# Attention with one ones-burst per block: pair sums folded by accumulating transfers

## The chip, the cores and the metric

The kernel runs on one core of one Trainium2 chip. The metric is the device time of that core in microseconds, from the start of the program to its end, as the median of several runs. The engines that matter here are TensorE (PE, matmuls into PSUM), ScalarE (ACT, exponentials and copies out of PSUM), VectorE (DVE, row maxima), GpSimd (POOL, sums of SBUF tiles) and SyncE (SP, which issues the transfers). Each engine runs its own instruction stream in order; they meet only through semaphores.

## What is computed

The reference is a state-space layer with a feed-forward layer, followed by one attention layer on x of shape (2, 2048, 512). The change touches only the attention, of which this is the core (16 heads of 32 columns, B = 2, N = 2048, D = 512):

```python
qkv = (h @ Wqkv.T + bqkv).reshape(B, N, num_heads, hd, 3)
q = jnp.moveaxis(qkv[..., 0], 2, 1)
k = jnp.moveaxis(qkv[..., 1], 2, 1)
v = jnp.moveaxis(qkv[..., 2], 2, 1)
energy = jnp.einsum('bhqd,bhkd->bhqk', q, k)
att = jax.nn.softmax(energy, axis=-1) / D ** 0.5
out = jnp.einsum('bhqk,bhkd->bhqd', att, v)
```

A softmax divides by the sum of the exponentials over all 2048 keys. How the kernel gets that sum is what is changed.

## The kernel before

The program is a series of stages with a barrier between them: preparation, state space, feed-forward, the projections to q, k and v, the attention, and the output projection. In the attention stage a *block* is 512 queries (CH) of one batch entry for a group of four heads (HG = 4). There are 4 groups x 2 entries x 4 chunks = 32 blocks. A block walks through 16 key *tiles* of 128 keys (NKT), and for each tile through four heads. `it` and `n` number the blocks: four blocks (n) to an iteration, eight iterations.

The work of a block, as it is spread over the engines:

- **TensorE** runs `one`. For each tile it does four `score` matmuls (keys x queries, 512 columns, L1554) into three PSUM banks in turn, and between them up to five `search` matmuls (L1540, three other banks) of the *following* block, whose row maxima have to be known before its scores. SHARES gives 4 searches in tile 0, 5 in tiles 1 to 12 and none in tiles 13 to 15 (here called the tail). Two tiles later (AV_LAG) it runs `weigh`, a burst of four matmuls (L1565), which multiplies the probabilities of a tile with the values. After every second tile it runs `total`, a burst of four matmuls with a tile of ones (L1575), which sums one pair of tiles over its 128 keys and accumulates in the PSUM bank DEN. Both bursts work on 32 output columns a head, in f32.
- **ScalarE** takes the exponential of each score bank into `probs` (L1650), eight buffers of four heads x 512. A buffer is free when `weigh` and the pair sum of its tile are done (`av_ready`, `pair_ready`). It also copies the two results, `o_sum` (L1632) and `den` (L1637), once a block.
- **GpSimd** adds the two `probs` tiles of a pair into `pair` (L1711), eight times a block, with two `pair` buffers; an add waits until `total` has read the buffer (`sums_ready`).
- **VectorE** reduces each search bank to row maxima (L1673, 64 a block), finishes the maxima, and in the tail inverts `den` (L1681) and multiplies it into `o_sum` (L1685).
- **SyncE** loads keys, values and queries of later blocks, the negated maxima (four small transfers of `load_max_rows`, L1062, which the first score of the next block waits for) and stores the results.

The order on each engine is the order of the code. `blocks` (L1432) runs block 0, then a hardware loop (`Fori`) of seven iterations with four blocks each, then the last three blocks; SyncE has a loop of its own over the groups. Waits inside the loops compare a semaphore with a count taken from the loop's register.

Of the kernel before, what the change touches and what calls it, by code (L numbers as in the profile page):

```python
# [6 lines left out]
P = 128  # L7
# [3 lines left out]
HEADS, HD = 16, 32  # L11
HG = P // HD
NG = HEADS // HG
CH = 512
# [1366 lines left out]
def attention_stage(nc, sb, sem, psum, a, wp, first, q_dram, k_dram, v_dram, att_dram):  # L1381
# [10 lines left out]
    NKT = L // P  # L1392
# [6 lines left out]
    NPROB = 8  # L1399
# [3 lines left out]
    AV_LAG, SUM_LAG = 2, 5  # L1403
# [7 lines left out]
    pair = [sb(f"pair{n}", [P, HG, CH]) for n in range(2)]  # L1411
# [9 lines left out]
    av_ready, pair_ready, sums_ready = sem("av_ready"), sem("pair_ready"), sem("sums_ready")  # L1421
# [10 lines left out]
    def blocks(engine, block):  # L1432

        block(0, 0, True, False)
        with engine.Fori(0, ITERS - 1) as it:
            for n in range(1, NB):
                block(it, n, False, False)
            block(it + 1, 0, False, False)
        for n in range(1, NB):
            block(ITERS - 1, n, False, n == NB - 1)  # L1440

    with nc.Block() as block:
        @block.sync
        def _(sp):
# [76 lines left out]
            group(0, True, False)  # L1521
            with sp.Fori(1, NG - 1) as g:
                group(g, False, False)
            group(NG - 1, False, True)
# [5 lines left out]
        def _(pe):  # L1530
# [12 lines left out]
            def score(it, n, kt, h):  # L1543

                if kt == 0 and h == 0:

                    pe.wait_ge(q_ld[n], (Q_LD + ROW_LD) * (it + 1))
                unit = UNITS * n + HG * kt + h

                if unit >= 3:  # L1550
                    pe.wait_ge(exp_ready, NB * UNITS * it + unit - 2)
                elif not (n == 0 and isinstance(it, int)):
                    pe.wait_ge(exp_ready, NB * UNITS * it)
                nc.tensor.matmul(psum[:, SC + unit % 3, :], keys[n // PB][0:R + 1, h, kt * P:(kt + 1) * P], queries[n][0:R + 1, h, :],  # L1554
                                 start=True, stop=True).then_inc(sc_ready, 1)

            def weigh(it, n, kt):

                tile = NKT * (NB * it + n) + kt
                pe.wait_ge(exp_ready, HG * (tile + 1))  # L1560
                if kt == 0:
                    pe.wait_ge(o_copied, NB * it + n + 1)
                    pe.wait_ge(v_ld[n // PB], 16 * (it // PER_GROUP + 1))
                for h in range(HG):
                    mm = nc.tensor.matmul(psum[h * HD:(h + 1) * HD, OUT, :], values[n // PB][:, kt, h * HD:(h + 1) * HD], probs[kt % NPROB][:, h, :],  # L1565
                                          start=(kt == 0), stop=(kt == NKT - 1))
# [17 lines left out]

            def pair_of(it, n, kt):

                return it, n, kt // 2

            def one(it, n, first, last):
                following = (it, n + 1) if n < NB - 1 else (it + 1, 0)  # L1590
                j = iter(() if last else range(MAXES))
                for kt in range(NKT):
# [21 lines left out]
                    if (kt - SUM_LAG) % 2 == 0 and (kt >= SUM_LAG or not first):  # L1614
                        total(*pair_of(*lagged(it, n, kt, SUM_LAG)))
# [4 lines left out]
            for kt in range(NKT + 1, NKT + SUM_LAG, 2):  # L1620
                total(ITERS - 1, NB - 1, (kt - SUM_LAG) // 2)

        @block.scalar
        def _(act):
# [9 lines left out]
            def copy_sums(count):  # L1634

                act.wait_ge(sums_ready, PAIRS * (count + 1))
                act.activation(den[:, :], psum[:, DEN, :], ACT.Copy).then_inc(den_copied, 1)  # L1637

            def one(it, n, first, last):
                count = NB * it + n  # L1640
                for kt in range(NKT):
                    tile = NKT * count + kt
                    if kt >= NPROB or not first:

                        act.wait_ge(av_ready, tile - NPROB + 1)
                        act.wait_ge(pair_ready, PAIRS * count + (kt - NPROB) // 2 + 1)
                    for h in range(HG):
                        act.wait_ge(sc_ready, HG * tile + h + 1)
                        unit = UNITS * n + HG * kt + h
                        act.activation(probs[kt % NPROB][:, h, :], psum[:, SC + unit % 3, :], ACT.Exp).then_inc(exp_ready, 1)  # L1650
                    if not first:
                        if kt == AV_LAG - 1:
                            copy_out(count - 1)
                        if kt == SUM_LAG - 1:
                            copy_sums(count - 1)
# [347 lines left out]
```

## Time and profile before

| | |
|---|---|
| median of 3 runs | 3516.28 us (3515.79 to 3516.89) |
| span of the profiled execution | 3515.4 us |
| mean granted TensorE clock | 0.966 of full speed |
| the attention stage in it | about 1452 to 3352 us |
| TensorE busy | 3268.0 us (93% of the span) |
| VectorE, ScalarE, GpSimd busy | 63%, 44%, 45% |

The profiled execution is 0.9 us under the median, so its durations can be set against the runs as they are. The busy time of TensorE is a modelled one, since matmuls are pipelined and overlap; for what a piece costs, the distance from one start to the next is the better measure. A block's length can be read as the distance between two copies of `o_sum` on ScalarE, of which there is one a block. A single `score` or `search` is 0.24 us from start to start in the dense part.

### The profile page before, as it was taken

The numbers are of one execution on the slowest core, as the hardware profiler recorded it, in microseconds if no ns is written. First come the engines' busy times: TensorE is split into PE (matmuls) and PEld (weight loads), VectorE is DVE, ScalarE is ACT, GpSimd is POOL, SyncE is SP. The second block draws the span as 40 slices with busy tenths as digits, with TensorE's granted clock in tenths as the row PEclk, the third lists the DMA queues.
The fourth block names the chain that finished last, engine by engine and source line by source line (L and its number), as shares of the span: only waits on it lengthen the run. The fifth ranks groups of instructions, "written<-read, shape, count | busy, mean of one in ns | idle before, by whom it ended". The sixth has DMA issues, their size and how long they took to land. (4 is left out here: it accounts for less than half of the span.)

```text
span 3515.4 us, 52215 instructions
## 1 busy us (share of the span) xinstructions
PE 3268.0 (93%) x16326; PEld 1933.5 (55%) x16326; DVE 2212.9 (63%) x3513; ACT 1553.0 (44%) x2770; POOL 1567.1 (45%) x538
## 2 busy tenths in 40 slices
PE   4786999999997989899999999999999999999976
PEld 2675777777875767544444444444444444444355
DVE  7884222222215446577778787777787777878558
ACT  2322232322222222465556555555555555655632
POOL 2665111100012111366566566666665565666655
PEclk8897999999998999999999999999999999999988
DMA  6233100000003463500122110122001230100044
GB/s 245 73 122 105 43 24 24 12 12 24 25 12 126 174 189 120 148 22 13 26 61 58 29 25 13 40 50 61 22 13 26 61 73 14 25 13 7 4 150 155
DMA packets 119434, 214.40 MB, mean 61 GB/s; under 512 B 11719, under 2 KB 29147, under 8 KB 118794
## 3 DMA queue, kind: packets, MB, share of 16 engines
q1 hardware_dynamic: 119180, 211.20, 20.0%
q8 instruction: 136, 2.23, 0.3%
q14 instruction: 118, 0.97, 0.1%
HBM read 135.34 MB, written 75.53 MB: 60 GB/s over the span
## 5 line engine op out<-in xcount | busy, mean ns | idle before, releaser
L1711 POOL TENSOR_TENSOR pair<-probs 128x2048 f32<-128x2048 f32 x256 | 1174.5, 4588 | 786.6 <-PE psum L1575 720.8
L1673 DVE TENSOR_REDUCE part_max<-psum 128x1 f32<-128x512 f32 x1984 | 1244.8, 685 | 387.8 <-PE psum L1540 387.8
L1650 ACT ACTIVATE probs<-psum 128x512 f32<-128x512 f32 x2048 | 1090.5, 599 | 787.0 <-PE psum L1554 786.5
L1554 PE MATMUL psum<-queries,keys 97*128 97x512 f32 x2048 | 817.8, 419 | 25.9 <-issue 11.8
L1540 PE MATMUL psum<-keys,queries 96*128 96x512 f32 x1984 | 834.0, 421 | 4.9 <-DMA queries<-q_parts 4.9
L1540 PEld LDWEIGHTS psum<-keys,queries 96*128 96x128 f32 x1984 | 377.5, 190 | 427.3 <-DVE part_max L1673 360.7
L1554 PEld LDWEIGHTS psum<-queries,keys 97*128 97x128 f32 x2048 | 378.4, 190 | 403.7 <-ACT probs L1650 332.6
L1565 PE MATMUL psum<-probs,values 128*32 128x512 f32 x4096 | 548.8, 608 | 0.0
L980 DVE TENSOR_TENSOR h_lo<-w_stage,h_hi 128x512 fp32r<-128x512 f32 x128 | 96.7, 756 | 528.4 <-ACT h_hi L918 528.4
L911 ACT ACTIVATE w_stage<-psum,b_col 128x512 f32<-128x512 f32 x128 | 88.2, 689 | 510.5 <-PE psum L38 510.5
L1024 POOL TENSOR_TENSOR ffn_u_lo<-ffn_u,ffn_u_hi 128x512 fp32r<-128x512 f32 x32 | 41.2, 1288 | 554.1 <-DVE ffn_u_hi L970 554.1
L1575 PE MATMUL psum<-pair,att_ones 128*32 128x512 f32 x2048 | 272.7, 605 | 2.2 <-POOL pair L1711 2.2
L36 PE MATMUL psum<-ffn_u_hi,w_hi 128*128 128x512 f32 x512 | 204.0, 398 | 6.4 <-DVE b_parts L1006 6.4
L36 PE MATMUL psum<-w_hi,h_hi 128*128 128x512 f32 x512 | 203.5, 398 | 0.0
L38 PE MATMUL psum<-ffn_u_lo,w_hi 128*128 128x512 f32 x512 | 203.0, 396 | 0.0
L37 PE MATMUL psum<-w_hi,h_lo 128*128 128x512 f32 x512 | 202.9, 396 | 0.0
L37 PE MATMUL psum<-ffn_u_hi,w_lo 128*128 128x512 f32 x512 | 202.9, 396 | 0.0
L38 PE MATMUL psum<-w_lo,h_hi 128*128 128x512 f32 x512 | 202.3, 395 | 0.0
L1565 PEld LDWEIGHTS psum<-probs,values 128*32 128x32 f32 x4096 | 80.9, 108 | 161.0 <-issue 88.5
L1371 POOL TENSOR_TENSOR qkv_u_lo<-qkv_u,qkv_u_hi 128x512 fp32r<-128x512 f32 x32 | 41.2, 1287 | 263.5 <-DVE qkv_u_hi L1316 263.5
L1681 DVE RECIPROCAL den<-den 128x512 f32<-128x512 f32 x32 | 107.2, 3350 | 47.1 <-ACT den L1637 47.1
L1337 DVE SCALAR_TENSOR_TENSOR qk_lo<-psum,bqkv_col,qk_hi 128x512 fp32r<-128x512 f32 x64 | 47.9, 750 | 118.7 <-ACT qk_hi L1266 118.7
(305 smaller groups left out, 3708.0 us busy)
## 6 DMA issues: line engine op xcount, KB each, us to landing
queries<-q_parts SPq DMA_DIRECT2D x96, 256.0 KB, 4.7
keys<-k_parts SPq DMA_DIRECT2D x42, 512.0 KB, 7.3
x<-in_x_dram SPq DMA_DIRECT2D x8, 1024.0 KB, 8.1
y<-in_x_dram SPq DMA_DIRECT2D x8, 1024.0 KB, 6.4
y_rows<-y SPq DMA_DIRECT2D x8, 1024.0 KB, 4.8
qkv_z<-z_rows SPq DMA_DIRECT2D x8, 1024.0 KB, 5.8
q_parts<-qk_hi SPq DMA_DIRECT2D x32, 256.0 KB, 2.0
q_parts<-qk_lo SPq DMA_DIRECT2D x32, 256.0 KB, 2.3
```

Source lines behind the costliest of these rows:

```text
L36: nc.tensor.matmul(out, w_hi, x_hi, start=first, stop=False)
L37: nc.tensor.matmul(out, w_lo, x_hi, start=False, stop=False)
L38: return nc.tensor.matmul(out, w_hi, x_lo, start=False, stop=last)
L980: dve.tensor_tensor(h_lo[j % NH][:, :], g[j % 2], h_hi[j % NH][:, :].bitcast(F32), ALU.subtract).then_inc(glo_ready, 1)
L1540: nc.tensor.matmul(psum[:, MX + j % 3, :], queries[n][0:R, h, qt * P:(qt + 1) * P], keys[n // PB][0:R, h, kc * CH:(kc + 1) * CH], start=Tr ...
L1554: nc.tensor.matmul(psum[:, SC + unit % 3, :], keys[n // PB][0:R + 1, h, kt * P:(kt + 1) * P], queries[n][0:R + 1, h, :], start=True, stop= ...
L1565: mm = nc.tensor.matmul(psum[h * HD:(h + 1) * HD, OUT, :], values[n // PB][:, kt, h * HD:(h + 1) * HD], probs[kt % NPROB][:, h, :], start= ...
L1575: mm = nc.tensor.matmul(psum[h * HD:(h + 1) * HD, DEN, :], ones[:, :], pair[p % 2][:, h, :], start=(p == 0), stop=(p == PAIRS - 1))
L1650: act.activation(probs[kt % NPROB][:, h, :], psum[:, SC + unit % 3, :], ACT.Exp).then_inc(exp_ready, 1)
L1673: dve.tensor_reduce(part_max[:, at, kc:kc + 1], psum[:, MX + j % 3, :], AX.X, ALU.max).then_inc(max_read, 1)
L1681: dve.reciprocal(den[:, :], den[:, :]).then_inc(inverted, 1)
L1711: pool.tensor_tensor(pair[p % 2][:, :, :], probs[2 * p % NPROB][:, :, :], probs[(2 * p + 1) % NPROB][:, :, :], ALU.add).then_inc(pair_read ...
```

## The change

The ones-matmuls are no longer done per pair. GpSimd still adds the two tiles of a pair. Then it issues a transfer from SBUF to SBUF that adds the previous pair buffer onto this one (`accum_op`, 128 x 2048 in f32, 1,024 KB), a *fold*. After seven folds the last pair buffer of the block holds the sum over all eight pairs, and `total` sums it over its 128 partitions in one burst, in tile 6 (SUM_KT) of the next block. Four `pair` buffers take the place of two and six `probs` buffers that of eight, so the SBUF used is the same. Six buffers do not divide the 16 tiles of a block evenly, so the blocks are written out for all engines and the loops are gone, SyncE's too.

```diff
-    NPROB = 8
+    NPROB, NPAIR = 6, 4
+    FOLDS = PAIRS - 1
-    AV_LAG, SUM_LAG = 2, 5
+    AV_LAG, SUM_KT = 2, 6
...
     def blocks(engine, block):
 
-        block(0, 0, True, False)
-        with engine.Fori(0, ITERS - 1) as it:
-            for n in range(1, NB):
-                block(it, n, False, False)
-            block(it + 1, 0, False, False)
-        for n in range(1, NB):
-            block(ITERS - 1, n, False, n == NB - 1)
+        for count in range(NB * ITERS):
+            block(count // NB, count % NB, count == 0, count == NB * ITERS - 1)
...
-            def total(it, n, p):
-
-                pe.wait_ge(pair_ready, PAIRS * (NB * it + n) + p + 1)
-                if p == 0:
-                    pe.wait_ge(den_copied, NB * it + n + 1)
+            def total(count):
+
+                pe.wait_ge(folded, 16 * FOLDS * (count + 1))
+                pe.wait_ge(den_copied, count + 1)
                 for h in range(HG):
-                    mm = nc.tensor.matmul(psum[h * HD:(h + 1) * HD, DEN, :], ones[:, :], pair[p % 2][:, h, :],
-                                          start=(p == 0), stop=(p == PAIRS - 1))
+                    mm = nc.tensor.matmul(psum[h * HD:(h + 1) * HD, DEN, :], ones[:, :],
+                                          pair[(PAIRS * count + PAIRS - 1) % NPAIR][:, h, :], start=True, stop=True)
                 mm.then_inc(sums_ready, 1)
...
+                    if kt == SUM_KT and not first:
+                        total(NB * it + n - 1)
                     searches()
                     score(it, n, kt, 2)
                     searches()
                     score(it, n, kt, 3)
                     searches()
-                    if (kt - SUM_LAG) % 2 == 0 and (kt >= SUM_LAG or not first):
-                        total(*pair_of(*lagged(it, n, kt, SUM_LAG)))
...
                         act.wait_ge(av_ready, tile - NPROB + 1)
-                        act.wait_ge(pair_ready, PAIRS * count + (kt - NPROB) // 2 + 1)
+                        act.wait_ge(pair_ready, (tile - NPROB) // 2 + 1)
...
                     pool.wait_ge(exp_ready, 2 * HG * (number + 1))
-                    if p >= 2 or not first:
-                        pool.wait_ge(sums_ready, number - 1)
-                    pool.tensor_tensor(pair[p % 2][:, :, :], probs[2 * p % NPROB][:, :, :], probs[(2 * p + 1) % NPROB][:, :, :],
-                                       ALU.add).then_inc(pair_ready, 1)
+                    if p >= NPAIR:
+                        pool.wait_ge(folded, 16 * (FOLDS * count + p - NPAIR + 1))
+                    elif not first:
+                        if p == NPAIR - 1:
+                            pool.wait_ge(sums_ready, count)
+                        else:
+                            pool.wait_ge(folded, 16 * (FOLDS * (count - 1) + PAIRS - NPAIR + p + 1))
+                    pool.tensor_tensor(pair[number % NPAIR][:, :, :], probs[2 * number % NPROB][:, :, :],
+                                       probs[(2 * number + 1) % NPROB][:, :, :], ALU.add).then_inc(pair_ready, 1)
+                    if p > 0:
+
+                        pool.wait_ge(pair_ready, number + 1)
+                        if p > 1 or not first:
+                            pool.wait_ge(folded, 16 * (FOLDS * count + p - 1))
+                        pool.dma_start(pair[number % NPAIR][:, :, :], pair[(number - 1) % NPAIR][:, :, :],
+                                       accum_op=ALU.add).then_inc(folded, 16)
```

How the change moves the instructions is seen on two engines. On GpSimd, at the start of the attention, block 0 stood so before (the number behind a name is the buffer):

```order
L1702 UNCONDITIONAL_BRANCH
L1711 TENSOR_TENSOR pair0<-probs0,probs1 128x2048
L1711 TENSOR_TENSOR pair1<-probs2,probs3 128x2048
L1711 TENSOR_TENSOR pair0<-probs4,probs5 128x2048
L1711 TENSOR_TENSOR pair1<-probs6,probs7 128x2048
```

Now the same place reads, up to the second add of block 1:

```order
L1690 UNCONDITIONAL_BRANCH
L1704 TENSOR_TENSOR pair0<-probs0,probs1 128x2048
L1704 TENSOR_TENSOR pair1<-probs2,probs3 128x2048
L1711 DMA pair1<-pair0 128x2048
L1704 TENSOR_TENSOR pair2<-probs4,probs5 128x2048
L1711 DMA pair2<-pair1 128x2048
L1704 TENSOR_TENSOR pair3<-probs0,probs1 128x2048
L1711 DMA pair3<-pair2 128x2048
...
L1704 TENSOR_TENSOR pair3<-probs2,probs3 128x2048
L1711 DMA pair3<-pair2 128x2048
L1704 TENSOR_TENSOR pair0<-probs4,probs5 128x2048
L1704 TENSOR_TENSOR pair1<-probs0,probs1 128x2048
```

Behind every add but a block's first there is a transfer on GpSimd's own queue, whose source is the destination of the transfer before it; two adds stand together where a block ends.

On TensorE, in the tail of block 0 (tiles 13 to 15) and at the jump into the loop, the order was:

```order
L1554 MATMUL psum<-queries,keys 128x512 x2
L1565 MATMUL psum<-probs,values 32x512 x4
L1554 MATMUL psum<-queries,keys 128x512 x2
L1575 MATMUL psum<-pair,att_ones 32x512 x4
L1554 MATMUL psum<-queries,keys 128x512 x2
L1565 MATMUL psum<-probs,values 32x512 x4
L1554 MATMUL psum<-queries,keys 128x512 x4
L1565 MATMUL psum<-probs,values 32x512 x4
L1554 MATMUL psum<-queries,keys 128x512 x2
L1575 MATMUL psum<-pair,att_ones 32x512 x4
L1435 UNCONDITIONAL_BRANCH
```

Now it is, up to the first searches of the next block:

```order
L1548 MATMUL psum<-queries,keys 128x512 x2
L1559 MATMUL psum<-probs,values 32x512 x4
L1548 MATMUL psum<-queries,keys 128x512 x4
L1559 MATMUL psum<-probs,values 32x512 x4
L1548 MATMUL psum<-queries,keys 128x512 x4
L1559 MATMUL psum<-probs,values 32x512 x4
L1548 MATMUL psum<-queries,keys 128x512 x3
L1534 MATMUL psum<-keys,queries 128x512
```

Both ones-bursts of the tail are gone, and so is the branch.

## Rows read from the trace of the kernel before

**Rows 1.** The page: busy time, the clock in 40 slices, and two groups.

```profile
PE 3268.0 (93%) x16326; PEld 1933.5 (55%) x16326; DVE 2212.9 (63%) x3513; ACT 1553.0 (44%) x2770; POOL 1567.1 (45%) x538
...
PEclk8897999999998999999999999999999999999988
...
L1711 POOL TENSOR_TENSOR pair<-probs 128x2048 f32<-128x2048 f32 x256 | 1174.5, 4588 | 786.6 <-PE psum L1575 720.8
...
L1575 PE MATMUL psum<-pair,att_ones 128*32 128x512 f32 x2048 | 272.7, 605 | 2.2 <-POOL pair L1711 2.2
```

**Rows 2.** Windows, the attention: busy by engine, granted clock, DMA share, GB/s.

```profile
1452.00:3352.00 1900.00, 1876.27 (x10159) 822.11 (x10158) 1465.07 (x2133) 1113.68 (x2105) 1174.52 (x256) 0.99 0.15 34
```

**Rows 3.** Waits from 1568 to 3304: total us, times, longest.

```profile
PE psum L1554 <- issue: 11.8, 6, 2.2
```

**Rows 4.** Timeline of ScalarE: the copies of `o_sum`; start, duration.

```profile
1686.43 0.60 ACT L1632 ACTIVATE o_sum<-psum 128x512 f32<-128x512 f32 x1
1751.93 0.61 ACT L1632 ACTIVATE o_sum<-psum 128x512 f32<-128x512 f32 x1
...
1870.20 0.61 ACT L1632 ACTIVATE o_sum<-psum 128x512 f32<-128x512 f32 x1
...
1929.32 0.60 ACT L1632 ACTIVATE o_sum<-psum 128x512 f32<-128x512 f32 x1
1990.44 0.60 ACT L1632 ACTIVATE o_sum<-psum 128x512 f32<-128x512 f32 x1
...
3303.45 0.60 ACT L1632 ACTIVATE o_sum<-psum 128x512 f32<-128x512 f32 x1
3346.94 0.60 ACT L1632 ACTIVATE o_sum<-psum 128x512 f32<-128x512 f32 x1 [1.89 <-PE psum L1565]
```

**Rows 5.** Timeline and windows around one jump of the loop.

```profile
1740.47 0.79 PE L1554 MATMUL psum<-queries,keys 97*128 97x512 f32 x1 [1.80 <-issue]
...
1736.00:1746.00 10.00, 8.20 (x35) 3.32 (x35) 4.12 (x4) 3.61 (x7) 6.00 (x2) 0.71 0.40 111
```

**Rows 6.** Timeline of a block's part with searches: three value bursts, five reductions.

```profile
1887.50 1.06 PE L1565 MATMUL psum<-probs,values 128*32 128x512 f32 x8
1889.04 3.08 DVE L1673 TENSOR_REDUCE part_max<-psum 128x1 f32<-128x512 f32 x5 [0.60 <-PE psum L1540]
1890.81 1.06 PE L1565 MATMUL psum<-probs,values 128*32 128x512 f32 x8
1895.30 1.06 PE L1565 MATMUL psum<-probs,values 128*32 128x512 f32 x8
```

**Rows 7.** Timeline of the same block's tail: value bursts and VectorE's product.

```profile
1913.75 1.06 PE L1565 MATMUL psum<-probs,values 128*32 128x512 f32 x8
1917.06 1.06 PE L1565 MATMUL psum<-probs,values 128*32 128x512 f32 x8
1918.42 3.35 DVE L1685 SCALAR_TENSOR_TENSOR att<-o_sum,den 128x512 f32<-128x512 f32 x1
1919.68 1.06 PE L1565 MATMUL psum<-probs,values 128*32 128x512 f32 x8
1923.48 1.06 PE L1565 MATMUL psum<-probs,values 128*32 128x512 f32 x8
```

**Rows 8.** Timeline of SyncE's queue in that tail: transfers issued.

```profile
1915.07 3.12 SPq L1062 DMA_DIRECT2D queries<-neg_rows  x4
...
1927.70 0.39 SPq L1454 DMA_DIRECT2D values<-v_rows  x1
```

**Rows 9.** DMA issues: count, KB each, median us from issue to landing.

```profile
values<-v_rows SPq DMA_DIRECT2D x8, 1024.0 KB, 10.9
...
out_dram<-p_result SPq DMA_DIRECT2D x7, 1024.0 KB, 4.3
...
queries<-neg_rows SPq DMA_DIRECT2D x128, 2.0 KB, 1.7
...
out_dram<-p_result SPq DMA_DIRECT2D x4, 256.0 KB, 2.2
```

More of the change, by code:

```diff
@@ L1410, in attention_stage @@
     probs = [sb(f"probs{n}", [P, HG, CH]) for n in range(NPROB)]
-    pair = [sb(f"pair{n}", [P, HG, CH]) for n in range(2)]
+    pair = [sb(f"pair{n}", [P, HG, CH]) for n in range(NPAIR)]
     part_max, neg_rows = first["part_max"], first["neg_rows"]
@@ L1420, in attention_stage @@
     sc_ready, exp_ready = sem("scores_ready"), sem("exp_ready")
-    av_ready, pair_ready, sums_ready = sem("av_ready"), sem("pair_ready"), sem("sums_ready")
+    av_ready, pair_ready, folded, sums_ready = sem("av_ready"), sem("pair_ready"), sem("pairs_folded"), sem("sums_ready")
     max_ready, max_read, turning, neg_ready = (sem(n) for n in ("max_ready", "max_read", "max_turning", "neg_ready"))
@@ L1519, in group @@
                         store(count - 1, g - 1, B - 1, NCH - 1)
[L1521 to L1524, printed above, removed]
+            for g in range(NG):
+                group(g, g == 0, g == NG - 1)
             store(B * NCH * NG - 1, NG - 1, B - 1, NCH - 1)
@@ L1551, in score @@
                     pe.wait_ge(exp_ready, NB * UNITS * it + unit - 2)
-                elif not (n == 0 and isinstance(it, int)):
+                elif it > 0:
                     pe.wait_ge(exp_ready, NB * UNITS * it)
@@ L1564, in weigh @@
                 for h in range(HG):
-                    mm = nc.tensor.matmul(psum[h * HD:(h + 1) * HD, OUT, :], values[n // PB][:, kt, h * HD:(h + 1) * HD], probs[kt % NPROB][:, h, :],
+                    mm = nc.tensor.matmul(psum[h * HD:(h + 1) * HD, OUT, :], values[n // PB][:, kt, h * HD:(h + 1) * HD], probs[tile % NPROB][:, h, :],
                                           start=(kt == 0), stop=(kt == NKT - 1))
                 mm.then_inc(av_ready, 1)
-            def total(it, n, p):
-                pe.wait_ge(pair_ready, PAIRS * (NB * it + n) + p + 1)
-                if p == 0:
-                    pe.wait_ge(den_copied, NB * it + n + 1)
+            def total(count):
+                pe.wait_ge(folded, 16 * FOLDS * (count + 1))
+                pe.wait_ge(den_copied, count + 1)
                 for h in range(HG):
-                    mm = nc.tensor.matmul(psum[h * HD:(h + 1) * HD, DEN, :], ones[:, :], pair[p % 2][:, h, :],
-                                          start=(p == 0), stop=(p == PAIRS - 1))
+                    mm = nc.tensor.matmul(psum[h * HD:(h + 1) * HD, DEN, :], ones[:, :],
+                                          pair[(PAIRS * count + PAIRS - 1) % NPAIR][:, h, :], start=True, stop=True)
                 mm.then_inc(sums_ready, 1)
@@ L1583, in lagged @@
                 return (it, n - 1, kt + NKT - lag) if n > 0 else (it - 1, NB - 1, kt + NKT - lag)
-            def pair_of(it, n, kt):
-                return it, n, kt // 2
             def one(it, n, first, last):
@@ L1619, in _ @@
                 weigh(ITERS - 1, NB - 1, kt - AV_LAG)
-            for kt in range(NKT + 1, NKT + SUM_LAG, 2):
-                total(ITERS - 1, NB - 1, (kt - SUM_LAG) // 2)
+            total(NB * ITERS - 1)
         @block.scalar
@@ L1634, in copy_sums @@
             def copy_sums(count):
-                act.wait_ge(sums_ready, PAIRS * (count + 1))
+                act.wait_ge(sums_ready, count + 1)
                 act.activation(den[:, :], psum[:, DEN, :], ACT.Copy).then_inc(den_copied, 1)
@@ L1649, in one @@
                         unit = UNITS * n + HG * kt + h
-                        act.activation(probs[kt % NPROB][:, h, :], psum[:, SC + unit % 3, :], ACT.Exp).then_inc(exp_ready, 1)
+                        act.activation(probs[tile % NPROB][:, h, :], psum[:, SC + unit % 3, :], ACT.Exp).then_inc(exp_ready, 1)
                     if not first:
@@ L1653, in one @@
                             copy_out(count - 1)
-                        if kt == SUM_LAG - 1:
+                        if kt == SUM_KT:
                             copy_sums(count - 1)
```

## Prediction

> **What bounds the kernel now.** I read the page first. TensorE is busy 93% of the span, and the granted clock is near full through the attention (slices 17 to 38) [rows 1]. Over the attention alone TensorE is busy 1876.27 of 1900 us and the DMA engines 0.15 of the time [rows 2]. Then the groups by line: the ones matmuls of L1575, 2048 records, which are 256 bursts of eight (four matmuls, each recorded twice), have 272.7 us [rows 1]. Then the waits: TensorE waits longest for "issue", 11.8 us in six pauses [rows 3]. So TensorE's order is the path, and each piece it loses shortens a block, until another chain takes over.
>
> The length of a block is the distance of two copies of `o_sum` by ScalarE: 1870.20 to 1929.32 is 59.1 us. At 1686.43 to 1751.93 it is 65.5 and at 1929.32 to 1990.44 61.1; the last block, which searches nothing, takes 43.5 [rows 4]. The long ones contain the loop's jump: a pause of 1.80 us in which TensorE waits for "issue". In the 10 us around that one the granted clock was 0.71, so it stood for a part of them at the lower of its two levels (1.2 GHz) [rows 5].
>
> **What is taken from TensorE.** Start to start, a tile with five searches and no ones-burst lasts 3.31 us (1887.50 to 1890.81), with one 4.49 (to 1895.30) [rows 6]. One burst costs 1.18. Six of the eight lie in the thirteen tiles with searches, and one is put back in tile 6: 5 x 1.18 = 5.9. The two others lie in the tail without searches, where ScalarE already holds the scores back: a tile takes 3.31 with a burst and 2.62 without (1913.75, 1917.06, 1919.68) [rows 7], so 0.7 there, and 0.9 for the last, whose 3.80 has a search too. Sum 7.5: TensorE alone would need 51.6 us a block.
>
> Cover for that: VectorE takes five searches in 3.08 us [rows 6], under the 3.31 of a tile; its last product of the tail ends at 1921.77, before the burst at 1923.48 ahead of which the searches begin again [rows 7]. The margin shrinks with the tail, but three free banks cover it: nothing. The loads of the negated maxima start at 1915.07 and take 3.12 us to issue, the last landing some 1.7 us later, near 1919.9 [rows 8, 9]; the scores that need them start about 1 us before the burst at 1923.48 now [rows 7], and 1.6 earlier then. Zero, if folds don't delay them by more than the 0.9 left; each further microsecond would cost 32.
>
> **The loop written out.** The intervals hold 6 jumps; above 59.1 they sum to 22 us (2.0 to 6.5 each, two of them with a slow clock) [rows 4]. Between the jumps, where the code is straight, there is no pause for "issue" [rows 3]: six, as many as the jumps. I take -22, and nothing for the longer program, which the trace does not price.
>
> **What is added: a serial chain.** In a block GpSimd now does add 0, add 1, fold 1, add 2, fold 2, ... add 7, fold 7, where fold p may be issued only when fold p-1 has landed, since it reads what that wrote. An add takes 4.59 [rows 1] and hides under the fold before. Let C be one fold's issue to the next one's. Six such steps, and between fold 7 and the next block's fold 1 two adds (9.2) and an issue (0.4, the price of one on SP's queue [rows 8]): the chain needs 6C + 9.6 a block. It hides below TensorE's 51.6 if C is at most 7.0, or 6.8 with the microsecond for other loads below. Below that nothing else bites: ScalarE needs pair p for tile 2p+6, two pairs (over 13 us) after its last exponential; the ones-burst in tile 6 comes some 20 us after the block's last exponential, an add and one or two folds fit in.
>
> No accumulating transfer, nor any issued by GpSimd, is in this trace. A fold reads 1,024 KB, reads the 1,024 KB it adds to, and writes 1,024 KB. From below: it costs no less than a plain transfer of the size, 4.3 us (`out_dram<-p_result`). From above: 10.9, as `values<-v_rows`, also 1,024 KB, beside other loads [rows 9]. Between them: SBUF to SBUF with hardly any bytes lands in 1.7 (`queries<-neg_rows`), and 768 KB more cost 2.1 (4.3 against 2.2), so 2.8 per 1,024 KB, while 4.3 less 1.7 is 2.6 and the mean transfer of this stage costs more: 0.15 x 1900 us for 34 GB/s x 1900 us is 4.4 us per 1,000 KB of the engines' time [rows 2, 9]. I take 3.1 a pass, in the lower part of 2.6 to 4.4. I count two passes, one for each operand read, the write beside them: 1.7 + 2 x 3.1 = 7.9, and 0.4 for the semaphore and the issue: C = 8.3. A gain from the fold itself is excluded; C lies in 4.7 to 11.3. I take this middle because the kind of work (reading both operands) is known and only its overlap isn't.
>
> The existing loads use 0.15 x 59.1 = 8.9 us of the DMA engines a block [rows 2], mostly issued at a block's start (the values at 1927.70 [rows 8]), where the chain has the slack of two adds. Between 0 and 6 us; I take 1.0.
>
> The Trainium skill (DMA: Bandwidth & Descriptors, Anatomy of one DMA) gives 2.0 us + bytes/436e3 for a transfer issued by GpSimd, and (Collectives: The Full Stack, The bandwidth ceiling: the fold count and why AG ≠ RS ≠ AR) says that an add in the DMA engines emits two read descriptors and runs at half a copy's rate. By these, a fold would be an estimated 2.0 + 2 x 2.4 = 6.8, just at the limit of 6.8, and the block would stay TensorE's, with the time of rival C below; no run here shows either figure.
>
> **Sum** (against the profiled span of 3515.4; the median of the runs is 0.9 more). Block: 6 x 8.3 + 9.6 + 1.0 = 60.4, 1.3 above 59.1; thirty such blocks +39. Jumps -22. The last block has no searches, so the chain stands out more: 6 x 8.3 + 9.6 - 43.5 = +16. Behind it the last ones-burst, which now waits for the last add alone, waits for one more fold: +8. First block +1. Together +42: 3557, as a run 3558. The slope is 30 x 6 + 6 + 1 = 187 us per microsecond of C; the break-even is C = 8.1.
>
> **Rivals.**
> A, the forecast: the chain sets the pace and is longer than what was taken away, C from 8.1 to 10.5: 3525 to 3970. For it: one pass alone has rows of 4.3. More may come on top: per pair TensorE would have 6.6 us of work in over 8, a pause of nearly 2 us each, and the pause of 1.80 came with a slow clock [rows 5]; four of the six jumps cost only 2.0 to 2.4 in all, so I add nothing. 0.42; a further 0.09 for C above 10.5 (at 11.3: 4119).
> B, the chain sets the pace, but C is 6.8 to 8.0: gain in part. At 7.5 it is 0.8 x 187 = 150 less than A: 3408. For it: the fixed 1.7 may overlap the issue; SBUF to SBUF has no HBM in it. 0.22.
> C, the chain is hidden, C at most 6.8. Thirty blocks x -7.5 = -224, jumps -22, last block 6 x 6.8 + 9.6 - 43.5 = +7, last fold +7, first block -5: -237, so 3279. Against it: a pass would have to cost 2.35 (1.7 + 2 x 2.35 + 0.4), below every row. 0.23.
> D, the chain's loss and the rest cancel within 0.2% (7 us, about what a measurement of this kernel tells from no change): C within 0.04 of 8.1. 0.04.
> That the change does not do what it says can be left out: the order shows one ones-burst a block.
>
> **How the numbers follow.** A is likeliest: 3558, its own range 3525 to 3970. The whole range takes in C's case below and leaves out the top of A and the very bottom: 3270 to 3960. Faster = B + C = 0.45, same 0.04, slower 0.42 + 0.09 = 0.51.
>
> **What would show it.** In the profile after: 256 - 224 = 32 bursts of ones; the landing time of `pair<-pair` (7.9 expected; under 6.4 is C, over 7.7 is A); GpSimd's adds waiting little for anything but behind the fold's wait, TensorE waiting for ScalarE and that for the pairs, once per pair; block distances of 60.4 with no long ones at every fourth; the last block near 60 rather than 43.5; DMA share up from 0.15 to about 0.8. Wrong would be: equal blocks near 52 (C), GpSimd's issue taking over 1 us of its own (it adds seven times per block), or a granted clock well below 1 through the attention, which would carry the time above 3960.

## The result, and the profile after

The changed kernel takes 3601.41 us (3597.51 to 3614.1, four runs) against 3516.03 of the kernel before in the same comparison: the ratio is 1.0252, with a 95% interval of 1.0232 to 1.0271. It is slower by 2.5%. The forecast was 3558, slower by 1.2%. The profiled execution has a span of 3595.7 us, 80.3 more than before.

The page after, its lines for [rows 1]: busy time, clock and DMA share in 40 slices, the two groups on GpSimd, and the issue of the folds.

```profile
PE 3131.7 (87%) x14534; PEld 1950.0 (54%) x14534; DVE 2251.0 (63%) x3513; ACT 1548.3 (43%) x2770; POOL 1760.0 (49%) x762
...
PEclk8888999999999999899998999898999889999978
DMA  6232000000004453866777767777677887666654
...
L1704 POOL TENSOR_TENSOR pair<-probs 128x2048 f32<-128x2048 f32 x256 | 1231.5, 4849 | 68.5 <-ACT probs L1638 68.5
...
L1711 POOL DMA_DIRECT2D pair<-pair x224 | 194.5, 868 | 601.5 <-DMA pair<-pair 576.4
...
pair<-pair POOLq DMA_DIRECT2D x224, 1024.0 KB, 7.1
```

And the windows over the attention, which answer to [rows 2], then the longest waits from 1568 to 3400 us, which answer to [rows 3].

```profile
1452.00:3432.00 1980.00, 1739.92 (x8351) 837.73 (x8349) 1502.89 (x2128) 1106.94 (x2101) 1365.81 (x480) 0.92 0.73 150
```

```profile
ACT probs L1638 <- PE psum L1548: 556.2, 486, 4.9
POOL pair L1711 <- DMA pair<-pair: 536.6, 175, 10.1
...
ACT probs L1638 <- POOL pair L1704: 151.4, 50, 9.5
PE psum L1548 <- ACT probs L1638: 121.8, 110, 7.8
...
PE psum L1568 <- DMA pair<-pair: 44.3, 22, 3.7
...
PE psum L1548 <- DMA queries<-neg_rows: 28.7, 11, 3.8
```

Read them in this order. TensorE has lost 136 us of busy time, and yet it is now idle for 12% of the attention. ScalarE's 556 us of waiting for scores say only that ScalarE is not the limit. GpSimd waits for hardly anything but its own transfers: 576 us for the folds, and only 68.5 us, in four places of the whole program, for ScalarE's exponentials. So a probability is there long before GpSimd takes it, and the pace is set by GpSimd and its folds. The rest of the chain can be read from the other waits: ScalarE waits for an add to free a `probs` buffer, TensorE waits for ScalarE to free a score bank. Twenty-two times TensorE waits in front of the one ones-burst for the last fold of the block before.

Where the 80.3 us lie is seen from the copies of `o_sum` and `den` on ScalarE, as in [rows 4].

```profile
1502.72 0.60 ACT L1620 ACTIVATE o_sum<-psum 128x512 f32<-128x512 f32 x1
...
1803.48 0.60 ACT L1620 ACTIVATE o_sum<-psum 128x512 f32<-128x512 f32 x1
...
1870.24 0.60 ACT L1620 ACTIVATE o_sum<-psum 128x512 f32<-128x512 f32 x1
...
3357.23 0.61 ACT L1620 ACTIVATE o_sum<-psum 128x512 f32<-128x512 f32 x1
...
3403.20 0.60 ACT L1620 ACTIVATE o_sum<-psum 128x512 f32<-128x512 f32 x1 [1.19 <-PE psum L1559]
3430.89 0.60 ACT L1625 ACTIVATE den<-psum 128x512 f32<-128x512 f32 x1 [27.09 <-PE psum L1568]
```

The first copy comes 6.4 us earlier than before (1509.13). Thirty blocks take (3357.23 - 1502.72) / 30 = 61.8 us each, where the same thirty took 59.8 with the loop's jumps in them: +60. The last block takes 46.0 (43.5 before), and its `den` comes 27.7 us behind its `o_sum`, where before it came 4.1 behind (3351.05): together +26. The sum is +80. The blocks are not alike: from 50.5 to 74.5 us, the one above 66.8.

What makes a long block shows on GpSimd's and SyncE's queues: the timeline of GpSimd, of SyncE and of TensorE around 1800 to 1843 us.

```profile
1799.52 1.19 SPq L1457 DMA_DIRECT2D queries<-q_parts  x2
...
1801.36 0.86 POOL L1711 DMA_DIRECT2D pair<-pair  x1 [3.46 <-DMA pair<-pair]
...
1801.87 0.39 SPq L1450 DMA_DIRECT2D values<-v_rows  x1
1801.97 4.86 POOL L1704 TENSOR_TENSOR pair<-probs 128x2048 f32<-128x2048 f32 x1
1802.30 13.17 SPq L1468 DMA_DIRECT2D att_columns<-att  x1
...
1815.37 0.87 POOL L1711 DMA_DIRECT2D pair<-pair  x1 [8.54 <-DMA pair<-pair]
...
1821.49 0.79 PE L1548 MATMUL psum<-queries,keys 97*128 97x512 f32 x1 [7.04 <-ACT probs L1638]
...
1835.44 0.87 POOL L1711 DMA_DIRECT2D pair<-pair  x1 [0.30 <-POOL pair L1704]
...
1842.92 0.87 POOL L1711 DMA_DIRECT2D pair<-pair  x1 [1.99 <-DMA pair<-pair]
```

From one fold's issue to the next, 1835.44 to 1842.92, is 7.48 us: that is C when nothing disturbs it, and some 80 of the 192 steps of the stage are 7.47 to 7.52. But the fold of 1801.36 shares the DMA engines with queries, 1,024 KB of values and a store, and the next one goes out 14.0 us later; TensorE then stands for 7.04 us. In this trace the distance over a block's end, with its two adds, is 10.2 to 10.3 us. An undisturbed block would be 6 x 7.49 + 10.25 = 55.2; the mean is 61.8. The difference, 6.6 us a block, lies in the steps between folds, and all but four of the steps end with the landing of the fold before (the four have GpSimd itself waiting for "issue", 7 us over 7.49 in all). What delays the landings is tested next.

### The profile page after: what moved, and what is told of

Read it like the earlier page. It is cut to its first block and busy times, and to the rows that moved or that the text cites. A ratio compares the mean times of both kernels' runs of the same rounds, so it can differ in the third digit from the quotient of the medians.

```text
span 3595.7 us, 40526 instructions
## 1 busy us (share of the span) xinstructions
PE 3131.7 (87%) x14534; PEld 1950.0 (54%) x14534; DVE 2251.0 (63%) x3513; ACT 1548.3 (43%) x2770; POOL 1760.0 (49%) x762
## 5 line engine op out<-in xcount | busy, mean ns | idle before, releaser
L1704 POOL TENSOR_TENSOR pair<-probs 128x2048 f32<-128x2048 f32 x256 | 1231.5, 4849 | 68.5 <-ACT probs L1638 68.5
L1548 PE MATMUL psum<-queries,keys 97*128 97x512 f32 x2048 | 841.7, 432 | 163.6 <-ACT probs L1638 129.1
L1534 PE MATMUL psum<-keys,queries 96*128 96x512 f32 x1984 | 871.2, 439 | 13.8 <-DVE part_max L1661 8.1
L1534 PEld LDWEIGHTS psum<-keys,queries 96*128 96x128 f32 x1984 | 397.1, 200 | 499.2 <-DVE part_max L1661 355.0
L1548 PEld LDWEIGHTS psum<-queries,keys 97*128 97x128 f32 x2048 | 403.8, 201 | 403.6 <-ACT probs L1638 280.1
L1559 PE MATMUL psum<-probs,values 128*32 128x512 f32 x4096 | 583.1, 643 | 2.3 <-ACT probs L1638 0.5
L1711 POOL DMA_DIRECT2D pair<-pair x224 | 194.5, 868 | 601.5 <-DMA pair<-pair 576.4
## 6 DMA issues: line engine op xcount, KB each, us to landing
keys<-k_parts SPq DMA_DIRECT2D x42, 512.0 KB, 10.5
```

Source lines behind the costliest of these rows:

```text
L1534: nc.tensor.matmul(psum[:, MX + j % 3, :], queries[n][0:R, h, qt * P:(qt + 1) * P], keys[n // PB][0:R, h, kc * CH:(kc + 1) * CH], start=Tr ...
L1704: pool.tensor_tensor(pair[number % NPAIR][:, :, :], probs[2 * number % NPROB][:, :, :], probs[(2 * number + 1) % NPROB][:, :, :], ALU.add) ...
L1711: pool.dma_start(pair[number % NPAIR][:, :, :], pair[(number - 1) % NPAIR][:, :, :], accum_op=ALU.add).then_inc(folded, 16)
```

## The experiments

### Where the block's 61.8 us come from

**e1_no_reloads**: the changed kernel, with the reloads of keys, queries and values within the attention replaced by counting their semaphores up. Its blocks all work on the first group's tiles.

```diff
-                        load_keys(g + 1, b, 0)
+                        sp.sem_inc(k_ld[b][0], 48)
...
-                        load_queries(g, place(w + NB)[1], n)
+                        sp.sem_inc(q_ld[n], Q_LD)
...
-                        load_values(g + 1, b)
+                        sp.sem_inc(v_ld[b], 16)
```

> The changed kernel with the reloads of keys, queries and values inside the attention left out (their semaphores are counted up, so every block works on the tiles of the first group; the output is not the reference's). Folds, bursts and stores stay. Theory M (GpSimd's chain of adds and folds sets the pace, and the reloads that share the DMA engines lengthen it): the fold steps fall to the undisturbed 7.5 us everywhere, a block to 6 x 7.49 + 10.25 = 55.2 from 61.8, so the run to about 3601 - 30 x 6.6 = 3400. Rival R1 (TensorE's lower clock, 0.93, or the waits for the maxima rows set the time, the reloads are hidden): no lower than 3570. In between would mean that something else joins the chain.

Measured: 3467.26 us, ratio to before 0.9866 (0.9846 to 0.9886); a block is 57.3 us in the mean. So the reloads cost 134 us, 4.5 a block, and the changed kernel without their collisions is faster than the kernel before: rival R1 falls. But theory M had asked for 55.2. Two microseconds a block stay. The waits of GpSimd are of the same kind as in the changed kernel (397.4 us for the folds, 2.0 for ScalarE), and what is left is again single long folds. One is seen here, in the timeline of GpSimd, the windows over it and the DMA queues from 1999 to 2009.

```profile
1999.37 0.87 POOL L1711 DMA_DIRECT2D pair<-pair  x1 [1.71 <-DMA pair<-pair]
...
2008.78 0.87 POOL L1711 DMA_DIRECT2D pair<-pair  x1 [3.93 <-DMA pair<-pair]
```

```profile
2003.00:2006.00 3.00, 3.00 (x17) 1.64 (x17) 2.77 (x5) 1.80 (x4) 1.85 (x1) 1.00 0.88 178
2006.00:2009.00 3.00, 3.00 (x18) 1.45 (x16) 2.77 (x6) 1.80 (x5) 0.22 (x1) 1.00 0.03 5
```

```profile
q0 software_dynamic: 144, 1.05, 52.3%
q8 instruction: 1, 0.02, 0.6%
q14 instruction: 1, 0.01, 0.2%
```

From 2006 on the DMA engines together are busy 0.03 of the time, with 5 GB/s, and the fold has still not landed. The packet records show more: fifteen engines finish with the fold between 2005.81 and 2005.97, and the last of its 8 KB packets starts only at 2006.80, as a 16 KB packet of an instruction queue ends that had begun at 2005.88. The fold lands at 2008.25. So a single engine of the sixteen is behind; that it is the one that moved the instruction packet is inferred from these times, since the records don't name the engine.

The same records sort all 224 folds by what else started between issue and landing: a packet of an instruction queue, or 20 KB or more of other transfers. The figures are the number of folds and their mean landing in us.

| | neither | other transfers alone | instruction packet alone | both |
|---|---|---|---|---|
| e1_no_reloads | 116, 6.96 | 25, 7.05 | 66, 7.72 | 17, 8.11 |
| changed kernel | 94, 6.96 | 53, 8.58 | 49, 7.56 | 28, 10.13 |

In e1 none of the 141 folds without an instruction packet took more than 7.23 us, so the stores of `att`, which are still there, delay nothing by themselves. That fetches of instructions cost these 2 us is therefore likely, but it is argued from a coincidence, and a fold that is late for another reason also has more time to meet such a packet. No run took the packets away.

**e2_plain_copy**: the fold as a plain transfer of the same size from the same queue, so that the last buffer holds the first pair only.

```diff
-                        pool.dma_start(pair[number % NPAIR][:, :, :], pair[(number - 1) % NPAIR][:, :, :],
-                                       accum_op=ALU.add).then_inc(folded, 16)
+                        pool.dma_start(pair[number % NPAIR][:, :, :], pair[(number - 1) % NPAIR][:, :, :]).then_inc(folded, 16)
```

> The changed kernel with the fold as a plain transfer of the same 1,024 KB from the same queue (no accumulate, so the sum holds only the first pair; the output is not the reference's). Theory M: the second operand's read is what makes a fold long, so a landing falls from 7.1 to about 4.5 us, the chain then needs less than TensorE's 51.6 us a block, and the run falls to 3270 to 3310. Rival R2 (the fold's length is GpSimd's own path: descriptors, issue, semaphore): landing stays within 0.5 us of 7.1 and the time near 3600.

**e3_half_fold**: an accumulating fold of two of the four heads, 512 KB, so that the sums of the other two heads are incomplete.

```diff
-                        pool.dma_start(pair[number % NPAIR][:, :, :], pair[(number - 1) % NPAIR][:, :, :],
+                        pool.dma_start(pair[number % NPAIR][:, 0:2, :], pair[(number - 1) % NPAIR][:, 0:2, :],
```

> The changed kernel with a fold of two of the four heads (512 KB, accumulating; the sums of two heads are incomplete, so the output is not the reference's). Theory M: of the 7.1 us about 1.9 are fixed and 5.2 go with the bytes, so landing is about 4.5 us and the run 3270 to 3320, set by TensorE. Rival R2 (fixed cost rules): landing over 6 us and the run over 3480.

Measured: e2 3291.67 us (0.9366, 0.9348 to 0.9385), e3 3285.04 us (0.9347, 0.9324 to 0.9371). The issue row of e2, and in its timeline two copies of `o_sum`:

```profile
pair<-pair POOLq DMA_DIRECT2D x224, 1024.0 KB, 4.7
```

```profile
2028.94 0.60 ACT L1620 ACTIVATE o_sum<-psum 128x512 f32<-128x512 f32 x1
2081.29 0.60 ACT L1620 ACTIVATE o_sum<-psum 128x512 f32<-128x512 f32 x1
```

and of e3:

```profile
pair<-pair POOLq DMA_DIRECT2D x224, 512.0 KB, 4.6
```

A plain 1,024 KB lands in 4.7, an accumulating 512 KB in 4.6, the fold in 7.1. So accumulating costs 2.4 us more than copying, of which 0.3 is the issue on GpSimd (0.57 us for the plain transfer, 0.87 for the fold), and about 2.1 of a fold do not depend on its size (4.6 x 2 - 7.1). Rival R2 falls. Both runs fell where theory M had put them, and both show the other chain: most blocks last 51.3 to 52.5 us (all of them 50.4 to 55.8), mean 52.2 and 51.9. TensorE's share of the sum was right; it was never reached.

**e4_loop_out**: the kernel before, with only its loops written out.

```diff
-        block(0, 0, True, False)
-        with engine.Fori(0, ITERS - 1) as it:
...
+        for count in range(NB * ITERS):
+            block(count // NB, count % NB, count == 0, count == NB * ITERS - 1)
```

> The kernel before with nothing changed but the loop over blocks (and SyncE's loop over groups) written out: eight probability and two pair buffers, a ones-burst per pair. The prediction's term: the six jumps and their two slow-clock stretches go, 22 us less, so 3494. Rival R3 (the longer straight program pauses for its own instructions, or the pauses move): 3510 to 3520, no change.

Measured: 3496.51 us (3491.85 to 3497.07), ratio 0.9946 (0.9929 to 0.9962). Two copies of `o_sum` in it:

```profile
1804.48 0.60 ACT L1625 ACTIVATE o_sum<-psum 128x512 f32<-128x512 f32 x1
1863.58 0.60 ACT L1625 ACTIVATE o_sum<-psum 128x512 f32<-128x512 f32 x1
```

All its thirty blocks but the last are 59.0 to 59.2; the long ones of [rows 4] are gone, with no pause of TensorE for "issue" left in the attention. The span is 21.3 us shorter. Rival R3 falls.

### What a fold may cost when nothing waits for it in series

**e5_two_chains** folds pair p onto pair p+2, with two semaphores, five `probs` and five `pair` buffers, and two ones-bursts. The fold itself is now issued so:

```diff
+                    if p > 1:
+                        pool.wait_ge(pair_ready, number + 1)
+                        if FOLDS * count + p // 2 - 1 > 0:
+                            pool.wait_ge(folded[p % 2], 16 * (FOLDS * count + p // 2 - 1))
+                        pool.dma_start(pair[number % NPAIR][:, :, :], pair[(number - 2) % NPAIR][:, :, :],
+                                       accum_op=ALU.add).then_inc(folded[p % 2], 16)
```

> The changed kernel with two chains of folds side by side: pair p is folded onto pair p+2, so a fold waits for the last but one (a semaphore for each chain), six folds a block, and the two last pair buffers are summed by two ones-bursts in tile 6. Five probability and five pair buffers, the same SBUF. Theory M (serial latency of the chain, 7.49 a step with collisions on top, was the pace; the DMA engines themselves have room: 6 x 5.3 + 9 us in a block): the chain is hidden again, TensorE's block is 51.4 + 1.1 = 52.5, and the run 3300 (3290 to 3330). Rival R4 (the DMA engines' throughput or GpSimd's adds beside the transfers are the limit, not the serial wait): block at 57 or more, run above 3450.

**e6_quads** has no chain: pair 0 onto 1, 2 onto 3, and so on, with a ones-burst for each of the four sums.

```diff
+                    if p % 2 == 1:
+                        pool.wait_ge(pair_ready, number + 1)
+                        if number > 1:
+                            pool.wait_ge(folded, 16 * (number // 2))
+                        pool.dma_start(pair[number % NPAIR][:, :, :], pair[(number - 1) % NPAIR][:, :, :],
+                                       accum_op=ALU.add).then_inc(folded, 16)
```

> The changed kernel with no chain at all: pair 0 is folded onto pair 1, 2 onto 3 and so on, four folds a block that do not wait for each other's sums, and four ones-bursts a block that accumulate. Six probability and four pair buffers, as changed. Theory M: every fold has two pairs' time (13 us), collisions with other transfers are absorbed, TensorE's block is 51.4 + 3 x 1.1 = 54.7, and the run 3365 (3350 to 3385). Rival R4 (DMA throughput): it would be better than two chains, since it moves a third less. Rival R5 (each burst costs less than 1.1 once the others are gone): nearer 3330.

Measured: e5 3460.53 us (0.9858, 0.9843 to 0.9873), block 57.4; e6 3411.65 us (0.972, 0.9707 to 0.9734), block 55.2 or up to 59.0, mean 56.0. Both beat the kernel before and both miss their figure, e5 by 160 us. GpSimd now waits for ScalarE (404 and 427 us), so the serial wait for the folds is gone. The numbers alone would fit rival R4, throughput: it had asked of e5 a block of 57 or more, and of e6 to be the better one. It is e11 below that excludes it. A new wait stands on TensorE: e5's waits from 1568 to 3250, then its timeline on SyncE, GpSimd and TensorE.

```profile
POOL pair L1705 <- ACT probs L1640: 404.4, 204, 7.1
...
PE psum L1548 <- DMA queries<-neg_rows: 90.2, 29, 4.5
```

```profile
2250.32 3.15 SPq L1062 DMA_DIRECT2D queries<-neg_rows  x4
2250.59 0.87 POOL L1711 DMA_DIRECT2D pair<-pair  x1 [0.33 <-POOL pair L1705]
...
2259.68 0.50 PE L1548 MATMUL psum<-queries,keys 97*128 97x512 f32 x1 [3.82 <-DMA queries<-neg_rows]
...
2261.13 1.94 PE L1559 MATMUL psum<-probs,values 128*32 128x512 f32 x8
```

Its issue row for the same transfers, with the median landing:

```profile
queries<-neg_rows SPq DMA_DIRECT2D x128, 2.0 KB, 5.5
```

Four transfers of 2 KB, the maxima rows of the next block, land in 5.5 us in the median where they took 1.7 [rows 9], while folds are in flight. TensorE stands for 3.8 us before its next score, and the burst behind it takes 1.94 us in place of 1.06: from 2259 to 2263 the granted clock was 0.67, so it stood for a part of them at the lower level. This is the margin of 0.9 us that the prediction named and priced at zero.

**e7_two_chains_early** and **e8_quads_early** tried to win that margin back by ending the searches a tile earlier, with a sixth place for a search at the end of a tile.

```diff
-    SHARES = [4] + [5] * 12 + [0] * 3
+    SHARES = [5] * 8 + [6] * 4 + [0] * 4
```

> The two-chain kernel with the searches of the next block finished one tile earlier: five in tiles 0 to 7, six in tiles 8 to 11, none in 12 to 15 (a sixth place for a search at the end of a tile). The maxima rows are then issued about 2.6 us earlier relative to the next block's first score. Theory M2 (in the two-chain kernel the 57.4 us block is TensorE's 52.5 plus the wait for the maxima rows, whose small transfers land in 5.5 us between the folds' packets, plus the slow clock after each such pause): the waits of TensorE for the maxima rows fall from 90 us to under 20, the block to 53 to 54, the run to 3340 (3310 to 3370). Rival R6 (the folds or GpSimd hold the block at 57 by themselves): no gain, 3450 to 3480.

> The kernel with four unchained folds and the same earlier searches. Theory M2: its waits for the maxima rows (43.8 us) go, but one more tile of the tail is held back by ScalarE (0.5 us a block): 55.7 a block everywhere, the run 3395 (3380 to 3410). Rival R6: no change, 3412, or slower, since six searches in a tile are VectorE's limit (6 x 0.62 = 3.7 against 3.55).

Measured: 3524.86 us (1.0036, 1.0022 to 1.005) and 3484.81 us (0.9922, 0.9908 to 0.9936). Both are 64 to 73 us slower than without the edit, and the waits for the rows are where they were (88.8 and 50.9 us). M2 falls in both; R6 had the slower outcome for e8, with its reason, and not for e7. Blocks are at least 57.9 and 57.2 us: a tile with six searches takes 3.90 us from burst to burst against 3.31 with five, though a search costs TensorE only 0.24; VectorE's six reductions, 0.62 each by [rows 6], need 3.7. And the rows were not sent earlier: in e7's timeline VectorE's small negation is held.

```profile
2204.25 4.56 POOL L1706 TENSOR_TENSOR pair<-probs 128x2048 f32<-128x2048 f32 x1 [2.05 <-ACT probs L1641]
...
2205.93 2.92 DVE L1055 TENSOR_SCALAR neg_rows<-max_rows 128x32 fp32r<-128x32 f32 x1
```

It takes 2.92 us in place of 0.2 (2.8 to 2.95 in 31 of the 32 blocks), and ends as GpSimd's add ends (2208.81); the next fold goes out right behind the rows again. The remedy was wrong; whether the folds hold the rows was still open, so the next runs kept a fold back.

**e9_quads_rows_first** is e6 with GpSimd waiting for the landed rows before it issues the fold of pair 5, and the bursts one tile later. **e10_chains_rows_first** is e5 with that wait ahead of pair 6, and **e11_chains_rows_at5** ahead of pair 5. Only e10 and e11 change the wait alone.

```diff
+                        if p == 5 and not last:
+                            after = count + 1
+                            pool.wait_ge(q_ld[after % NB], (Q_LD + ROW_LD) * (after // NB + 1))
```

> The kernel with four unchained folds, and in each block GpSimd issues the fold of pair 5 only after the four small transfers of the next block's maxima rows have landed (today it issues it 0.2 us after they start, in front of them on the same DMA engines); the ones-bursts stand one tile later (tiles 2, 6, 10, 14), so the late fold is not waited for. Theory M3 (the fold in flight is what holds the rows back): landing of the rows falls from 3.8 to about 1.8 us, TensorE's waits for them from 43.8 us to near 0, with them the slow clock behind them; every block 55.2, the run 3412 - 25 = 3387. Rival R7 (the rows are late by themselves, through VectorE or the shorter tail): waits stay near 40 us and the run near 3412.

> The two-chain kernel with the same wait ahead of the fold of pair 6. Theory M3: of the two folds that are in flight when the rows are sent one is gone, so their landing falls from 5.5 to 3 to 4 us and TensorE's waits for them from 90 to about 40 us; block from 57.4 to about 55, run about 3380. Rival R7: waits stay at 90 us and the run at 3460; or the delayed fold makes the ones-burst of tile 6 wait, which would show as TensorE waiting for pair<-pair.

> The two-chain kernel with the wait for the maxima rows ahead of the fold of pair 5 and not of pair 6: in the trace of the former it was pair 5's fold that was issued 0.35 us after the rows' transfers began, so the former kept the wrong fold back. Theory M3: rows land in 2 to 3.5 us (pair 4's fold may still run), TensorE's waits for them fall from 86 to under 30 us, block 53 to 54, run 3310 to 3360. Rival R7 (the rows are late whatever the folds do, or two chains keep the DMA engines too full): 3430 or more.

Measured: e9 3351.46 us (0.9537, 0.9524 to 0.9551), e10 3455.75 (0.9838, 0.9824 to 0.9852), e11 3330.07 (0.9479, 0.9466 to 0.9492). In e10 the fold that stood right behind the rows was pair 5's and not pair 6's, a misreading of mine; nothing moved (85.7 us of waits). With pair 5's fold held back, the rows land in 1.7 and 1.8 us. The rows of e9, one block's end and its issue row:

```profile
2196.59 2.40 SPq L1062 DMA_DIRECT2D queries<-neg_rows  x4
...
2200.68 0.87 POOL L1713 DMA_DIRECT2D pair<-pair  x1 [4.15 <-DMA queries<-neg_rows]
```

```profile
queries<-neg_rows SPq DMA_DIRECT2D x128, 2.0 KB, 1.7
```

and the waits of TensorE in e11, then windows of 1500 to 3150 us, of e5 and of e11:

```profile
PE psum L1548 <- DMA queries<-neg_rows: 0.9, 3, 0.4
```

```profile
1500.00:3150.00 1650.00, 1545.50 (x7787) 769.01 (x7786) 1337.15 (x1975) 992.67 (x1888) 1195.34 (x401) 0.95 0.68 143
...
1500.00:3150.00 1650.00, 1598.77 (x8360) 785.31 (x8356) 1333.01 (x2067) 1069.42 (x2043) 1302.27 (x437) 1.00 0.73 153
```

TensorE no longer waits for them, the granted clock is 1.00 through these windows (0.95 in e5), and the blocks are 54.2 (e9) and 53.4 us (e11) in the mean. M3 holds in e9 and e11, and R7 falls there. e10's own forecast, 3380, failed with the misreading: it doesn't speak against M3, nor for it. R4 falls with e11, which moves the same six folds a block as e5, keeps the DMA engines busier (0.73 against 0.68), and is 130 us faster. e9 came out 36 us better than expected: it had taken 55.2 for a block free of stalls, but in e6 every block had one (31 waits). By e9's 54.0 a burst costs (54.0 - 51.4) / 3 = 0.9 us, which speaks for R5; how much of e9's gain is the moved bursts is not shown. e11 is 184 us, 5.2%, faster than the kernel before. Its blocks still range from 52.2 to 56.8, and no run tested the long ones.

## Why the prediction was half right

**What bounded the kernel, and what left TensorE: right.** TensorE alone was to need 51.6 us a block; most blocks of e2 and e3 have 51.3 to 52.5 when the fold is short.

**The loop's jumps, -22: right.** e4 shortens the span by 21.3 us, and the run by 18 (13 to 25 by the interval of its ratio).

**The chain as the pace (rival A): right.** GpSimd waits for folds and almost never for ScalarE; shortening the fold (e2, e3) brings the time to 3290, as rival C had it.

**The step that failed is the term for other transfers**: "Between 0 and 6 us; I take 1.0". What delays the folds measured 6.6 us a block. By e1 the reloads are 4.5 of it, inside the bounds but 3.5 above what was taken. The reason given, that they are issued where the chain has the slack of two adds, is not what the trace shows: with seven folds a block the DMA engines are busy 0.73 of the time, and a batch of loads lasts longer than the slack: from 1801 to 1816, while the one fold above was in flight, SyncE's queue moved 2.30 MB. The other 2.1 are a term that the sum did not have: landings that are late beside instruction packets. Such packets were there before as well (254 in the whole run, 167 now), but the kernel before has no chain of transfers for them to delay.

**The price of a fold was off the other way**, and hid part of that. C was taken as 8.3 and is 7.49 undisturbed (an issue of 0.87 included, which I had at 0.4); a pass over an operand costs 2.4 to 2.6 us by e2 and e3, not 3.1. That is -4.9 a block, the two adds and their issue +0.65 (10.25 for 9.6), the other transfers +5.6: +1.4 on a forecast of 60.4, or 42 us for thirty blocks. The miss is 43 in the runs (3601 against 3558) and 38 in the spans (80 against 42). In the spans the rest is this: the end came 2 us later than forecast, and the first copy of `o_sum` 6.4 us earlier than before where I had +1; what made it earlier is open. With C alone corrected, and 1.0 for the others, the forecast would have been rival B, faster than before. So the sign was right partly because two errors opposed each other.

Put in the Trainium skill's terms (DMA: Bandwidth & Descriptors, Anatomy of one DMA, and Collectives: The Full Stack, The bandwidth ceiling), 2.0 us + 2 x 2.4 for a fold gave an estimated 6.8. By that rule the trace agrees within 5%: 7.0 to 7.1 to landing, and 2.4 for the second read, where the rows that I used came from transfers through HBM. The prediction weighed the rule as a rival. The chain was not hidden even so: from issue to issue an undisturbed fold takes 7.49, about half a microsecond more than to its landing, and the limit was 7.0.

**The end of the stage, +24: right in size.** It is +26: the last block 2.5 longer, and `den` 23.6 later behind it. I had put 16 on the block and 8 on the fold; ScalarE and TensorE run ahead and the whole delay shows behind `o_sum`.

**The maxima rows, zero: wrong in principle, hidden here.** TensorE waits 28.7 us for them in the changed kernel, in 11 blocks, but off the path, since GpSimd sets the pace. In seven of the eleven the slowest of the four transfers lands in 4.1 to 7.4 us; in the four others (10.5 us of the waits) they land in 1.6 to 2.6, and it is the negation ahead of them that is held: it takes 2.9 to 5.4 us. One of the four, with the add that it ends with:

```profile
2668.56 5.36 DVE L1055 TENSOR_SCALAR neg_rows<-max_rows 128x32 fp32r<-128x32 f32 x1
2669.01 4.85 POOL L1704 TENSOR_TENSOR pair<-probs 128x2048 f32<-128x2048 f32 x1
```

The prediction names neither the negation nor a price for it. As soon as the chain is broken up (e5, e6) they are the next bound, worth 60 us (e9) and 130 us (e11).

What stays open: whether fetches of instructions cause the last 2 us a block in e1. The stores of `att` alone delayed no fold there, but no run took the fetches away.

## What to carry to other kernels

A serial chain of transfers is priced by its step in company, not alone: at a DMA share of 0.73 a step of 7.49 us took (61.8 - 10.25) / 6 = 8.6 in the mean, and in e11, at the same share, a block takes 53.4 us although a fold there lands in 8.6 in the median, because no fold waits for the one just before it. So break the chain first: independent folds, or two chains. And after adding bulk transfers look for the smallest transfer that someone waits for: here 2 KB, sent 0.3 us ahead of 1,024 KB on another queue, cost 60 us with four folds and 130 with two chains, while the choice between these two schemes is worth 49 us or, with the rows first, 21.

## What the runs showed of the hardware

- An accumulating transfer of 1,024 KB within SBUF lands in 6.9 to 7.2 us undisturbed, a plain one in 4.7 in the median (e2), an accumulating 512 KB in 4.6 (e3). Issuing takes 0.87 us of GpSimd's own time for an accumulating one of either size, and 0.57 for the plain one.
- GpSimd's add holds some VectorE operations until it ends. The negation of 32 columns takes 0.2 us alone and 2.92 beside an add (e7), up to 5.36 in the changed kernel; the product of L1685, 3.35 us in [rows 7], takes 0.69 in e9, where GpSimd waits at that moment. The reciprocal of `den` takes 3.34 us beside an add or not, and the adds beside these operations are no longer than the others. The Trainium skill (SBUF — State Buffer, Who interferes with whom) says that a VectorE operation with two SBUF inputs contends with a GpSimd instruction that reads SBUF, and that one with at most one such input contends only in a two-port mode, which a tensor_scalar can enter and in which whoever issues first blocks the other. By that rule, the trace agrees for the product, the reciprocal and the negation of e7. Three negations of the changed kernel began 0.3 to 0.5 us before the add, while GpSimd was issuing a fold, and were held to the add's end all the same. No run shows VectorE holding an add.
- A fold is late by 0.6 to 0.8 us in the mean when a packet of an instruction queue, and nothing else, starts between its issue and its landing (7.56 and 7.72 against 6.96); in the case shown it waited for one engine of sixteen for over 2 us.
- A loop's jump cost TensorE a pause of 1.8 to 2.2 us each time; two of the six long blocks were 4 us longer still, the one in [rows 5] with a granted clock of 0.71.
